# Cross-attention and experts on one core: scores by query as short row-tiled products, three buffers of query blocks, the mask in a row of the keys

## The reference

```python
def xattn(q_in, k_in, v_in, key_padding_mask, Wq, bq, Wk, bk, Wv, bv, Wo, bo):
    q, k, v = (q_in @ Wq + bq), (k_in @ Wk + bk), (v_in @ Wv + bv)      # split in 16 heads of 8
    score = jnp.einsum('bhqd,bhkd->bhqk', q, k) / jnp.sqrt(8.0)
    score = jnp.where(mask, -1e30, score)
    attn = jax.nn.softmax(score, axis=-1)
    return jnp.einsum('bhqk,bhkd->bhqd', attn, v)... @ Wo + bo
x = x + xattn(layernorm(x), ctx_1024, ctx_1024, mask, ...)
x = x + ffn(layernorm(x), Wr, W1, b1, W2, b2)    # softmax router, top 2 of 8, gelu(h @ W1 + b1) @ W2 + b2
```

## Time and profile before

| what | us |
|---|---|
| median of three runs | 844.66 |
| their range | 834.1 to 855.23 |
| the profiled execution, by its device time | 847.77 |
| its span, first to last instruction | 846.0 |

### The profile page before, as it was taken

How to read it: one execution, slowest core, us unless ns; L and a number is a source line. 1 busy time by engine, 2 the same in 40 slices (tenths; PEclk the granted TensorE clock), 3 DMA queues, 4 the chain that set the end, 5 groups by cost and what they waited for, 6 DMA issues and landing times.

```text
span 846.0 us, 18252 instructions
## 1 busy us (share of the span) xinstructions
PE 658.2 (78%) x4964; PEld 494.5 (58%) x4964; DVE 554.3 (66%) x1813; ACT 528.3 (62%) x1060; POOL 492.4 (58%) x892
## 2 busy tenths in 40 slices
PE   1787888878888988888888376998888898988500
PEld 0455666656566666666565255876776686766400
DVE  4556778867877778687875454666555565646436
ACT  3466776856776767667776265877666676858300
POOL 8233376665757666676768642675654565665710
PEclk9879999989998999999999578999999999999855
DMA  4756667666766576566751368876666756664069
GB/s 139 211 165 188 209 209 238 187 186 191 231 193 190 190 229 209 171 204 179 222 167 61 94 217 258 253 234 196 205 195 192 220 181 195 215 207 132 10 243 352
DMA packets 118905, 164.24 MB, mean 194 GB/s; under 512 B 22479, under 2 KB 77286, under 8 KB 118823
## 3 DMA queue, kind: packets, MB, share of 16 engines
q1 hardware_dynamic: 88711, 126.14, 48.3%
q10 hardware_dynamic: 21024, 20.06, 8.3%
q0 software_dynamic: 9088, 17.07, 6.4%
HBM read 73.07 MB, written 33.92 MB: 126 GB/s over the span
## 4 chain that ended last, share of the span: by engine, by line
PE 53%; issue 13%; ACT 8%; DMA 7%; POOL 6%; ACTq 6%; DVE 4%; SPq 2%; another core or an unknown queue 1%; POOLq 0%; DVEq 0%
ACTq L1069 5%; PE bank L1261 5%; PE bank L1249 4%; PE bank L1276 4%; PE bank L1429 4%; PE bank L1427 4%; PE bank L1428 4%; PE bank L1412 3%; PE bank L1415 3%; PE bank L1413 3%; DMA qb<-yd 3%; PE bank L1189 3%; PE bank L1216 2%; ACT pt L997 2%; POOL xd L538 2%
## 5 line engine op out<-in xcount | busy, mean ns | idle before, releaser
L638 POOL DMA_INDIRECT yd<-vs,idt x156 | 159.5, 1022 | 129.4 <-DVE vs L949 84.5
L538 POOL DMA_INDIRECT xd<-rows,posi x128 | 128.9, 1007 | 104.9 <-DVE posi L800 75.2
L935 DVE TENSOR_TENSOR qb<-hid,qb 128x512 fp32r<-128x512 f32 x156 | 108.3, 694 | 105.6 <-ACT hid L1143 68.4
L695 DVE TENSOR_REDUCE mx<-bank 128x4 f32<-128x480 f32 x256 | 159.7, 649 | 26.4 <-PE bank L1249 19.6
L997 ACT ACTIVATE pt<-bank,mcol 120x512 f32<-120x512 f32 x256 | 168.5, 692 | 10.2 <-PE bank L1261 10.1
L1140 ACT ACTIVATE qb<-bank,btile 128x512 fp32r<-128x512 f32 x156 | 109.1, 699 | 80.1 <-PE bank L1429 55.7
L1261 PE MATMUL bank<-qb,dense 128*120 128x512 f32 x256 | 103.6, 470 | 11.6 <-issue 4.5
L1143 ACT ACTIVATE hid<-bank,btile 128x512 f32<-128x512 f32 x156 | 108.8, 697 | 0.0
L1029 ACT ACTIVATE ots<-bank 128x512 f32<-128x512 f32 x64 | 38.2, 598 | 102.5 <-PE bank L1276 36.8
L1249 PE MATMUL bank<-kb,dense 128*128 128x480 f32 x256 | 88.8, 428 | 7.2 <-DVE mx L695 3.4
L1276 PE MATMUL bank<-pt,vs 120*32 120x128 f32 x2048 | 72.8, 282 | 1.5 <-issue 1.4
(11 more groups left out here) (169 smaller groups left out, 1559.7 us busy)
## 6 DMA issues: line engine op xcount, KB each, us to landing
kb<-wd SPq DMA_DIRECT2D x40, 512.0 KB
qb<-wd SPq DMA_DIRECT2D x38, 512.0 KB
qb<-dense SPq DMA_DIRECT2D x128, 128.0 KB
dense<-comp SPq DMA_DIRECT2D x64, 248.0 KB
kb<-dense ACTq DMA_DIRECT2D x128, 120.0 KB
rows<-xd SPq DMA_DIRECT2D x39, 264.0 KB
wd<-wsp SPq DMA_DIRECT2D x16, 512.0 KB
qb<-yd SPq DMA_DIRECT2D x16, 512.0 KB, 6.0
```

Source lines behind the costliest of these rows:

```text
L538: g.indirect_dma_start(xd, bass.IndirectOffsetOnAxis(ap=posi[r % 4][:, bk:bk + 1], axis=0), rows[r % 4][:, bk // 2, bk % 2, :], None, boun ...
L638: g.indirect_dma_start(yd, bass.IndirectOffsetOnAxis(ap=idt[k][:, j:j + 1], axis=0), yrow[p.parity][:, j, :], None, bounds_check=2 * NTOK ...
L695: v.tensor_reduce(mx[c % 2][:, :, gg, b], wide[m % 2][:, 0:J * KL].rearrange("p (j k) -> p j k", j=J), op=ALU.max, axis=AX.X).then_inc(w_f ...
L935: v.tensor_tensor(hhl[:, 1, c, :], hid[:, c % 2, :], hhl[:, 0, c, :], ALU.subtract).then_inc(h_lo, 1)
```

## The change

The key blocks are gone, with ACT's DMAs, the two `kb` tiles and their clearing. `by_query` takes its operands straight from `dense`: each head is a product of its own over 32 rows (a row tile of the array), with 128 query columns as weights and 120 key columns moving. A call takes one sample and two heads j, over four g: eight products, alternating between two row tiles and between the two `wide` banks. There are four calls a chunk in place of eight products. The call waits until both banks are free, and both are released with its last two products. The `best` reductions keep their number and size. `qb` has three buffers, and SP fills them one slot earlier, `mask_rows` too, which now writes the mask into a pad row of each head in `dense`, where it serves both kinds of product; so the exponential has no bias. The one-rows and the rows of the maxima are moved within the 32. The experts' weight tiles, which lay in `kb` and one `qb`, lie in two `qb`, and their split inputs in a tile of their own.

```diff
-    NHI, NLO, MSK = 3, 7, 11
+    MSK, NLO, NHI = 11, 15, 31
+    NB = 3
-        qb = [sb(f"qb{k}", [P, J, G, N2], F32R) for k in range(2)]
-        kb = [sb(f"kb{k}", [P, J, G, K2], F32R) for k in range(2)]
+        qb = [sb(f"qb{k}", [P, J, G, N2], F32R) for k in range(NB)]
...
             def mask_rows(c):
+                if c < ND:
+                    sp.wait_ge(dense_set, 2 * (c + 1))
+                else:
+                    sp.wait_ge(b_full, 8 * (c - ND + 1))
                 if c == 0:
                     sp.wait_ge(mask_dram, 16)
-                sp.wait_ge(kfirst[c % 2], 16 * (c // 2 + 1))
-                sp.dma_start(kb[c % 2][MSK:MSK + 1]...to_broadcast([1, G * J, K2])).then_inc(mask_row[c % 2], 16)
+                sp.dma_start(dense[c % ND][MSK::R, :, N2:NK]...to_broadcast([J, G, K2])).then_inc(mask_row[c % ND], 16)
             def query_blocks(c):
-                if c < 2:
-                    sp.wait_ge(qb_zero, c + 1)
+                if c < NB:
+                    sp.wait_ge(qb_zero[c], 1)
                 else:
-                    sp.wait_ge(b_full, 8 * (c - 1))
+                    sp.wait_ge(b_full, 8 * (c - NB + 1))
+                sp.wait_ge(dn_in[c % 2], 64 * (c // 2 + 1))
...
             def slot(n):
-                if chunk(n + 1):
-                    query_blocks(n + 1)
+                if chunk(n + 3):
+                    mask_rows(n + 3)
                 if chunk(n + 2):
-                    mask_rows(n + 2)
+                    query_blocks(n + 2)
...
-            v.memset(flat(kb[0], "p j g n").bitcast(F32), 0.0).then_inc(kb_zero, 1)
+            v.memset(flat(qb[2], "p j g n").bitcast(F32), 0.0).then_inc(qb_zero[2], 1)
...
-                if n == -3:
-                    v.memset(flat(kb[1], "p j g n").bitcast(F32), 0.0).then_inc(kb_zero, 1)
...
-                             bias=mcol[:, 2 * c + t // G:2 * c + t // G + 1], scale=SCALE).then_inc(exp_done, 1)
+                a.activation(pt[i % NP][:]..., scores[t % 2][0:KL, :], ACT.Exp, scale=SCALE).then_inc(exp_done, 1)
...
-            def key_blocks(c):
-                ...
-                if chunk(n + 2):
-                    key_blocks(n + 2)
...
-            def by_query(c, u):
+            def by_query(c, p):
                 if not chunk(c):
                     return
-                b, g = divmod(u, G)
-                if u == 0:
-                    pe.wait_ge(kblk[c % 2], 48 * (c // 2 + 1))
-                    pe.wait_ge(mask_row[c % 2], 16 * (c // 2 + 1))
-                m = 8 * c + u
-                if m >= 2:
-                    pe.wait_ge(w_free, m - 1)
-                t_.matmul(wide[m % 2][:, 0:J * KL]..., dense[c % ND][:, g, b * S:(b + 1) * S],
-                          kb[c % 2][:, :, g, b * KL:(b + 1) * KL], start=True, stop=True).then_inc(w_full, 1)
+                b, half = divmod(p, 2)
+                if p == 0:
+                    pe.wait_ge(dn_in[c % 2], 64 * (c // 2 + 1))
+                    pe.wait_ge(mask_row[c % ND], 16 * (c // ND + 1))
+                m = 8 * c + 2 * p
+                if m:
+                    pe.wait_ge(w_free, m)
+                for g in range(G):
+                    for k in range(2):
+                        j = 2 * half + k
+                        last = t_.matmul(wide[k][:, g * KL:(g + 1) * KL], dense[c % ND][R * j:R * j + R, g, b * S:(b + 1) * S],
+                                         dense[c % ND][R * j:R * j + R, g, N2 + b * KL:N2 + (b + 1) * KL], start=True, stop=True, tile_position=(R * j, 0))
+                        if g == G - 1:
+                            last.then_inc(w_full, 1)
...
             def slot(n):
-                by_query(n + 1, 4)
-                by_query(n + 1, 5)
+                by_query(n + 1, 2)
...
-                by_query(n + 1, 6)
-                by_query(n + 1, 7)
+                by_query(n + 1, 3)
...
-                by_query(n + 2, 1)
...
-                by_query(n + 2, 2)
-                by_query(n + 2, 3)
+                by_query(n + 2, 1)
```

More of the change, by code:

```diff
@@ L44, in turns, with moe_attention @@
         return self.quad * each + (each + more)
-def moe_attention(nc, x, ctx, mask, maskT, Wq, Wk, bqk, Wv, bv, Wo, bo, Wr, W1, b12, W2, out):
+def moe_attention(nc, x, ctx, mask, Wq, Wk, bqk, Wv, bv, Wo, bo, Wr, W1, b12, W2, out):
     S, B, D = x.shape
@@ L104, in moe_attention @@
         bias_qk = sb("bias_qk", [P, 2])
-        ones_k = sb("ones_k", [P, 1])
+        pad_q = sb("pad_q", [P, 1])
+        pad_k = [sb(f"pad_k{i}", [P, 1]) for i in range(3)]
         masku = sb("masku", [B, KL], mask.dtype)
@@ L176, in moe_attention @@
         flat = lambda t, spec: t[:].rearrange(f"{spec} -> p ({spec[2:]})")
[L177 to L181, removed]
+        wtile = [flat(qb[1 + k // 2], "p j g n")[:, k % 2 * 4 * HID:(k % 2 + 1) * 4 * HID].rearrange("p (k w n) -> p k w n", k=2, w=2) for k in range(4)]
+        xTh, xTl = ([xThl[:, k, i, :] for k in range(2)] for i in range(2))
         hhl = flat(qb[0], "p j g n").rearrange("p (k c t) -> p k c t", k=2, c=HC)
@@ L201, in moe_attention @@
         w_in, w_in2, wqk_in, bias_in = (sem(k) for k in ("w_in", "w_in2", "wqk_in", "bias_in"))
-        dense_set, kb_zero, qb_zero, pad_set = sem("dense_set"), sem("kb_zero"), sem("qb_zero"), sem("pad_set")
+        dense_set, qb_zero, pad_set = sem("dense_set"), [sem(f"qb_zero{k}") for k in range(NB)], sem("pad_set")
         x_in, ctx_in = four("x_in"), [sem(f"ctx_in{k}") for k in range(NC)]
-        mask_in, mask_f, mask_dram, mcol_done = sem("mask_in"), sem("mask_f"), sem("mask_dram"), sem("mcol_done")
-        mask_row = two("mask_row")
+        mask_in, mask_f, mask_dram = sem("mask_in"), sem("mask_f"), sem("mask_dram")
+        mask_row = four("mask_row")
         ident_done, bo_done, half_done, vs_zero = sem("ident_done"), sem("bo_done"), sem("half_done"), sem("vs_zero")
@@ L211, in moe_attention @@
         w_full, w_free = sem("w_full"), sem("w_free")
-        dn_in, qblk, kblk, kfirst, mrow = two("dn_in"), two("qblk"), two("kblk"), two("kfirst"), two("mrow")
+        dn_in, qblk, mrow = two("dn_in"), [sem(f"qblk{k}") for k in range(NB)], two("mrow")
         v_full, v_taken = sem("v_full"), sem("v_taken")
@@ L873, in _ @@
             dve.wait_ge(ident_done, 2)
-            v.tensor_tensor(ones_k[:, :], ident[:, NHI:NHI + 1], ident[:, NLO:NLO + 1], ALU.add).then_inc(pad_set, 1)
+            v.tensor_reduce(pad_q[:, :], ident[:, MSK::R], op=ALU.add, axis=AX.X).then_inc(pad_set, 1)
+            v.tensor_reduce(pad_k[0][:, :], ident[:, NHI::R], op=ALU.add, axis=AX.X).then_inc(pad_set, 1)
+            v.tensor_reduce(pad_k[1][:, :], ident[:, NLO::R], op=ALU.add, axis=AX.X).then_inc(pad_set, 1)
+            dve.wait_ge(pad_set, 3)
+            v.tensor_tensor(pad_k[2][:, :], pad_k[0][:, :], pad_k[1][:, :], ALU.add).then_inc(pad_set, 1)
             put(v.memset(mv[:], 1.0))
@@ L977, in _, with clear @@
             a = nc.scalar
-            def clear(blocks):
-                a.activation(flat(blocks, "p j g n"), ident[:, P - 1:P].to_broadcast([P, J * G * N2]), ACT.Copy, scale=0.0).then_inc(qb_zero, 1)
+            def clear(k):
+                a.activation(flat(qb[k], "p j g n"), ident[:, P - 1:P].to_broadcast([P, J * G * N2]), ACT.Copy, scale=0.0).then_inc(qb_zero[k], 1)
             for k, w in ((0, Wq), (1, Wk)):
@@ L985, in _ @@
             act.wait_ge(ident_done, 2)
-            clear(qb[0])
+            clear(0)
             def exponential(c, t):
@@ L1261, in by_key @@
                 t_.matmul(scores[t % 2][0:KL, :].rearrange("p (j q) -> p j q", j=J), dense[c % ND][:, g, N2 + b * KL:N2 + (b + 1) * KL],
-                          qb[c % 2][:, :, g, b * S:(b + 1) * S], start=True, stop=True).then_inc(b_full, 1)
+                          qb[c % NB][:, :, g, b * S:(b + 1) * S], start=True, stop=True).then_inc(b_full, 1)
             def weigh(w):
@@ L1456, in laid_out @@
         'ctx': a['ctx_1024'].transpose(2, 0, 1),
-        'mask': a['mask_BxS2_bf0'], 'maskT': a['mask_BxS2_bf0'].T,
+        'mask': a['mask_BxS2_bf0'],
         'Wq': a['L0_xattn_Wq'][:, cols], 'Wk': a['L0_xattn_Wk'][:, cols],
```

45 lines of the change are left out of this document (15 added, 30 removed).

## The result

The changed kernel takes 928.17 us (median of four runs) where the kernel before, run beside it, takes 846.1: a ratio of 1.103 (95% interval 1.084 to 1.122). The forecast was 818 and faster. The kernel before itself takes 802 to 805 us in four of the five sets of runs of the experiments and 844.7 in the third, so every run is compared with the kernel before of its own set.

A forecast was written before the change was run, and what follows sets the result against it. PE and ACT were taken to alternate as the limit. Per slot -1.2 - 0.44 + 0 + 0.9 = -0.7 us, -22 over 31 slots, start -5: -27 us, 818 on the median; range 798 to 868, the forecast's own 806 to 828.

The forecast's parts named there:

- ACT's relief: ACT's queue in the attention slots: removing four issues per chunk gains 1.2 plus 0.44 us per slot.
- The 5 at the start: Start of the kernel: the clearing of `kb` by DVE and ACT's first issues go, gaining 5 us, ends 2 and 8.
- The short products: PE's by_query calls: four overlapped rounds of two tiles cost 0.44 us, as the two long products did; net 0.
- Rival 1: by_query calls: loads of the two row tiles follow each other, 1.76 us more per slot, 28 slower, 873; chance 0.19.
- The switches: PE around by_query calls: entering and leaving the tiled form, six sides of 0.2 us, taken as 0.9 per slot.
- 0 on the path: DVE's reductions: start some 0.3 us later, four times, but slack covers it; cost 0, upper end 1.2 us.
- PE's own stall: PE, once per slot: a 1 us stall no other engine causes, growing by up to 0.2 us with more instructions.
- a higher granted clock: PE's clock: a higher granted clock was listed among the signs that the forecast is right; no size given.

The follow-up runs named there:

- e4: Kernel before without ACT's four issues for the key blocks, products by query waiting for the spread's landing instead: 749.69 us (0.936).
- e4b: e4 repeated in the fourth set, the kernel before without the copies of key blocks: 749.79 us (0.931).
- e5: Changed kernel with the two loops of a by_query call exchanged, four products of the first head, then four of the second: 775.68 us (0.968).
- a_again: The changed kernel once more, unaltered, in the second set, where the kernel before takes 801.7 us: 775.83 us (0.969).
- e1b: Changed kernel with two untiled products per by_query call in place of eight row-tiled ones, second set: 752.28 us (0.939).
- e2b: Changed kernel with PE's `earlier` moved behind by_key 2 and 3, second set: 764.95 us (0.954).
- e9: Kernel before with key blocks issued by SP behind `query_blocks` in place of ACT, and `mask_rows` after the loads: runs of 843.4 and 856.1 us.
- e1: Changed kernel with two untiled products of 128 rows by 480 columns per by_query call in place of eight row-tiled ones, first set: 752.96 us (0.940).
- e2: Changed kernel with PE's `earlier` moved behind by_key 2 and 3, first set: 754.92 us (0.942).
- e7: Changed kernel with `earlier` moved as in e2 and the third by_query call's increments held until `turn_rows`' first transpose: runs of 919.5 and 935.8 us.
- e6b: Changed kernel with the third by_query call's two increments given only by `turn_rows`' first transpose, from the fourth chunk on, fourth set: 902.81 us (1.121).

## Why the prediction was wrong

**ACT's relief: right.** The forecast gave it 1.64 us per slot and 5 at the start, 56 us. e4 and e4b, which do it alone, gain 52 and 55. The 5 at the start aren't seen in the changed kernel: its first by_key starts at 39.6 us against 39.0 before (35.8 in e4).

**The short products: right in the number.** The rounds of two take 0.11 us as taken from the column tiles, a call 0.587 us from first start to the next line's. The Trainium skill's page "TensorEngine Tiling (Array Packing)", "Key Properties", says that different tiles can load and multiply in parallel; the trace is in line with it, with loads of two tiles every 0.11 us. But in e5 both loads of a pair belong to one tile and the pace is the same, so it isn't shown that the pairs come from the tiles being different, as the forecast supposed. Rival 1, whose direction was met, had the wrong mechanism, and its 873 us lie below the 928.

**The switches: nearly right.** 0.9 us per slot forecast, 0.88 measured (a_again against e1b), which holds all that the tiled form costs. From the start of the instruction in front of a call to that of the one behind it, a_again needs 0.23 us more than e1b before `turn_on` and 0.16 before `weigh`, two of each per slot: 0.77 us. The rest is the longer wait at `earlier`. The forecast was a slot 0.7 us shorter and 27 us in all; where the kernel before takes 801.7 the change gives 26 us. That the sum is met so closely is in part luck: nothing came at the start, and the slot gained a little more than forecast (26 us over 31 slots are 0.84).

**DVE: wrong by its step "0 on the path".** I counted DVE's slack and not who waits for it: `best` 4 and 5 stand in front of `route` 3, and PE's `earlier` waits for that. At `earlier` PE stood 26.4 us in the 18 slots of the result's 300 us and 23.1 in 24 slots of a_again, where the kernel before has 5.4 in 9. Where the kernel before takes 801.7, moving `earlier` gains 10.9 us (e2b against a_again), so there it is a size missed, not the cause of the loss; with holds it becomes the longer of PE's two stands.

**PE's own stall: the step that failed.** I had it as "a stall of PE's own that no other engine causes", 1 us per slot and growing at most by 0.2 with the instructions. What I did not see: increments made shortly before it are held too, 1.8 us in the slot shown, and in the kernel before this is mostly hidden because the one who waits, `take_heads`, stands behind the four issues. I had that very wait in the earlier trace rows and read it as the issues' cost alone. In the changed kernel the hold meets the increments for DVE (166.20 to 168.04) in 26 slots, on a path that ends at PE. The sum took PE's stall as unchanged but for 0.2 us, and gave no price to whom it would hit. Why the hold moved from `weigh` to by_query isn't shown: ACT's relief, the form of the products and the later reductions changed together, and e9, which has the first alone, keeps its clock.

**The clock: the term left out.** I forecast "a higher granted clock", since ACT's waits vanish. Of the 4.3 us between 12.8 (a_again's steady slots) and 17.1 us per slot, the half clock is about 3.4 (6.8 us at half speed, in the stretch from 170.6, with PE busy all through it), and 0.9 are left for the hold itself; this split is an estimate. The runs with the hold made by hand say something near it: 17.1 to 14.4 us, 2.7 for the clock when the stands are filled. No term of the forecast could have given this: the range ended at 868 with every cost added up at full clock.

**What stays open.** What holds PE's increments, and why often where the kernel before takes 846 us and hardly where it takes 802. The sets ran on chips 0, 6, 2, 1 and 1, and only the one on chip 2 had many holds, so it may be the chip; the result's chip isn't on record. Fetches of instructions, which the trace has as queues 8 and 14, fall on 9 of the 28 stretches in which increments are held in the result's attention stage, and on 4 of 31 before, so they don't explain them. Traces with many holds lack three tenths of the records of semaphore updates (12,641 in the result against 18,152 in a_again), so the recording itself may be what stands in the way, but no run here tells. e1, e2 and e4 were not run where holds are frequent. That the loss belongs to hold and wait rests on the result's trace and on the hold made by hand, which gives its clock and its slots, though with longer stands of PE.

**The best version.** e2, the changed kernel with `earlier` two products later, computes the whole and takes 755 to 766 us where the kernel before takes 802 to 805 and the changed one 776. It was not run where the kernel before takes 846; with a hold by hand on top, e7 took 919.5 there, 9% more than the kernel before, about what the changed kernel lost.

## What to carry to other kernels

When an engine is relieved, ask what its old delay was covering: list every wait that ended under it, with its length, and give the longest of them a price as if it were bare. In a loop that PE bounds, a wait of PE is not worth its own length only: here stands of 0.6 and 1.5 us in a slot cost about 3.4 us more by the clock, so compare the granted clock by stretches as soon as slots are longer than any engine's work. And where a kernel's own time differs by 5% between sets of runs, the gain of a change may have the other sign there: this one lost 10% and gained 3%.

## What the runs showed of the hardware that was not expected

A loop can lock to the clock: slots of 17.0 to 17.1 us in two different kernels, 22 in a row in e6b and 14 in all, at most 6 in a row, in the result, 10.3 us at full and 6.8 at half clock, though PE's stands differ in length. More work made the kernel faster: five filling matmuls per slot, 903 to 830 us. Products of one and the same row tile overlap in pairs as those of two tiles do (0.60 against 0.59 us for eight). And increments of semaphores by PE can arrive 1.8 us after the matmul's end, with short stands of PE in the middle of unrelated matmuls meanwhile.
